# Window attention and box normalisation: x transposed in four equal pieces, 49 weight columns for the values, both normalisations moved

## The chip, the cores and the metric

The kernel runs on one core of a Trainium2 chip. The metric is device time in microseconds, the median of the runs. Such a core has a matrix engine (TensorE, PE in the profile, with its weight loads as PEld), VectorE (DVE), ScalarE (ACT), GpSimd (POOL) and a queue engine SyncE (SP), which issues the transfers. They work in parallel, each through its own instructions in order, and meet by semaphores. TensorE writes to PSUM, which is split in banks.

## The reference

x has 32 images of 56 x 56 tokens with 96 channels. Two layers, each with a residual.

```python
# _gn: group normalisation, 32 groups of 3 channels, over a whole image
x = x + attention(_gn(x))      # layer 1
x = x + box_layer(_gn(x))      # layer 2

# attention: x rolled by (-3, -3), cut into 64 windows of 7 x 7 = 49 tokens
qkv = xw @ qkv_w.T + qkv_b                     # 12 heads of 8 channels
attn = einsum(q * d**-0.5, k) + bias + mask    # 49 x 49 for each window and head
out = softmax(attn) @ v;  out = out @ proj_w.T + proj_b     # rolled back

# box_layer: s = x summed over 5 neighbours along a row
num = box_sum(s * s, channels, 20)
denum = box_sum(box_sum(x * x, row, 5), channels, 20) * count
out = nan_to_num(num / denum, nan=1.0)
```

## The kernel before

The order of all work is written out by hand. Every engine runs the same loop over slots (`for s in range(FIRST_SLOT, END_SLOT + 1)`, from -78 to 1070). A step j is a pair of windows; its scores are computed in slot j - 1. A unit U is one row of windows (four steps, four slots), an image is eight units (32 slots), and a group G is eight rows of image tokens in layer 2, seven to an image. The constants at the top (lines 44 to 53) say in which slot, counted from the start of a unit or an image, each piece of work stands: `units(s, V_AT)` gives the unit whose values are due in slot s, and so on. All pieces of a unit thus recur every four slots, and a slot is named below by its number modulo 32, or modulo 4 where it is the same in every unit.

Work of one unit on its way: `load` (SP) brings 112 x 4 x 96 tokens into one of eight `tok_in` tiles. `turn_x` (TensorE, line 377, L387) transposes them into bankA in four pieces, three of 112 tokens and one of 56. ScalarE's `keep_x` (L627) copies them to X, VectorE takes statistics (L869), and GpSimd splits X into a high and a low bf16 part, XH and XL (L991, L997). `qk` (L394 to L396) projects into bankB and bankC with the weights WH and WL, in three bf16 products each. ScalarE and VectorE split the results again (L635, L637; low_q L821, low_k L827), and SP's `stage` copies them into KS, QS and KE (L317, L325, L330), two units at a time. `values` (line 417, L436) computes v with 64 columns of XH or XL as weights at a time, although a window has 49 tokens: 48 products a unit, into the two halves of bankA; `keep_v` (L646) copies them.

Each step runs through `scores` (L454), `add_bias` (VectorE, L808), `maximum` (L815), `shift` (GpSimd, L1036), `turn_scores` (L466), `exponentials` (ScalarE, L656) and `times_v` (L481). For each unit follow `invert_sums` and `divide_o` (L838, L845), `turn_o` (L494), `keep_o` (L665), `project_o` (L504, into bankB) and `add_residual` (L857).

Layer 2 of a group: `normalise` to Y (ScalarE, L733), three sums on GpSimd (L1001, L1006, L1013), `square` and `square_box` (ScalarE, L740, L747), `deep_squares` (L549), `wide_squares` and `deep_y` (L555, L566), `invert` (L760, L763), `scale_squares`, `scale_boxes` and `ratio` (VectorE, L887, L894, L900), `turn_x1` (L575), `result` (L907), `store`. They stand in slots Y_AT to STORE_AT, four slots apart for successive groups.

Each normalisation is a chain across engines with links in fixed slots: aggregate (VectorE, L876), mean (L510) and variance (L515) on TensorE, deviation (L676 to L680), root (L687, L689) and scale (L699 to L713) on ScalarE. The first goes on to the weights: `norm_weights` multiplies them by the scale (L522, in bankA, the last work of TensorE's slot), `high_weights` on ScalarE writes the high part (L720, L724), and `fold` on VectorE the low part (L881, L882). `fold` comes first in VectorE's slot, ahead of `add_bias`.

What sets the order around the change: bankA passes in every unit from `values` (slot 0 modulo 4) to `turn_x` (slot 2) to `turn_o` (slot 3), and a normalisation's link uses it after the values have been kept. bankB passes between `qk` (slot 1), `deep_squares` (slot 2), `wide_squares` (slot 3) and, after `ratio` has read it, `project_o` (slot 0). `qk` waits for `add_residual` to have read bankB. TensorE's order in a slot is scores, times_v, values, turn_x, turn_o, turn_scores, turn_x1, project_o, qk, deep_squares, wide_squares and deep_y, and last the normalisation's links.

Of the kernel before, what the change touches and what calls it, by code (L numbers as in the profile page):

```python
# [8 lines left out]
BF16 = mybir.dt.bfloat16  # L9
ALU = mybir.AluOpType  # L10
# [33 lines left out]
LOAD_AT, FILL_AT, STATS_AT, HIGH_AT, LOW_AT = -78, -50, -49, -27, -27  # L44
# [4 lines left out]
Y_AT, PAIR_AT, FOUR_AT, BOX_AT = 45, 46, 47, 48  # L49
SQ_AT, DEEP_AT, WIDE_AT, RATIO_AT, OUT_AT, STORE_AT = 49, 50, 51, 52, 53, 54  # L50

NORM1 = dict(aggr=-21, mean=-20, dev=-20, var=-19, root=-19, scale=-18, weights=-16, high=-16, fold=-15)
NORM2 = dict(aggr=39, mean=40, dev=40, var=41, root=41, scale=42)
# [74 lines left out]
def build(nc, x, wT, bias_row, pT, pb_row, flipped, consts, out):  # L128
    ctx = ExitStack()
    with ctx:  # L130
# [20 lines left out]
        WH = sb("WH", [C + 1, 2 * C], BF16)  # L151
        WL = sb("WL", [C + 1, 2 * C], BF16)
# [143 lines left out]
        def _(sp):  # L296
# [43 lines left out]
            sp.dma_start(K[:, :], consts).then_inc(consts_in, 16)  # L340
            for U in range(UNITS):
                load(U)
# [8 lines left out]
            sp.wait_ge(pool_fills, 1)  # L351
# [23 lines left out]
        def _(pe):  # L375

            def turn_x(U):
# [7 lines left out]
                for t in range(4):  # L385
                    n = 2 * SIDE if t < 3 else SIDE
                    mm = pe.transpose(bankA[0:C, 2 * SIDE * t:2 * SIDE * t + n], tok_in[U % LOADS][0:n, t, :],  # L387
                                      roll[0:n, 0:n])
                mm.then_inc(xT_made, 1)

            def project(dst, col, u, done):

                xs = slice(TOK * u, TOK * u + TOK)
                pe.matmul(dst[0:C, 0:TOK], WH[:, col:col + C], XH[:, xs], start=True, stop=False)  # L394
                pe.matmul(dst[0:C, 0:TOK], WH[:, col:col + C], XL[:, xs], start=False, stop=False)
                pe.matmul(dst[0:C, 0:TOK], WL[:, col:col + C], XH[:, xs], start=False, stop=True  # L396
                          ).then_inc(done, 1)

            def qk(U):
# [9 lines left out]
                project(bankB, 0, u, q_made)  # L409
# [5 lines left out]
                project(bankC, C, u, k_made)  # L415

            def values(U):
# [10 lines left out]
                for w in range(2):  # L428
                    for p in range(PAIRS):
                        at = TOK * u + L * (2 * p + w)  # L430
                        xh, xl = XH[:, at:at + 64], XL[:, at:at + 64]
                        col = (2 * p + w) * C // 2
                        for part, (lhs, rhs) in enumerate(((xh, WHV), (xh, WLV), (xl, WHV))):
                            for h in range(2):
                                wv = rhs[m % 2][:, :].rearrange("c (a h d) -> c a h d", h=2, d=D)
                                mm = pe.matmul(bankA[64 * h:64 * h + 64, col:col + C // 2], lhs, wv[:, :, h, :],  # L436
# [179 lines left out]
        def _(act):  # L616
# [98 lines left out]
            def high_weights(m):  # L715
                act.wait_ge(norm_pe[0], PE_LINKS[0] * m + 3)
                if m:

                    act.wait_ge(k_made, UNITS * m)
                norm_link(m, 0, 13, act.activation(WH[:, :], bankA[0:C + 1, 0:2 * C], ACT.Copy))  # L720
# [370 lines left out]
```

## Time and profile before

| | us |
|---|---|
| median of 3 runs | 3615.91 (3614.39 to 3616.12) |
| profiled execution, its own time | 3616.91 |
| its span | 3615.1 |
| TensorE busy | 3343.9 (92%) |
| VectorE busy | 2800.6 (77%) |
| ScalarE busy | 2400.4 (66%) |
| GpSimd busy | 2276.4 (63%) |
| granted TensorE clock, mean | 0.988 |

The busy times say how much work each engine has, not which of them sets the end. The row of 40 slices says that the work is even from the second slice to the last but two. For the path one has to look at the timeline of one unit: which instruction starts late, and which engine it has waited for. In the timeline a row gives the start, the duration (of all instructions merged in the row, to the end of the last), the engine, the line, output <- input, shapes, the count, and in brackets the idle time before it with what ended it.

### The profile page before, as it was taken

What the parts mean: (1) busy time and instruction counts of PE and PEld (TensorE: products, weight loads), DVE (VectorE), ACT (ScalarE), POOL (GpSimd) and SP (SyncE); (2) the same over time, 40 slices, a digit from 0 to 9 for tenths busy, and PEclk for the clock granted to TensorE, in tenths of its full rate; (3) what the DMA queues carried; (4) which work ended last, traced back from release to release, by engine and by line L of the source; (5) the groups of instructions that cost most, each with busy time, mean ns of one, the idle gap of its engine ahead of it and who ended that gap; (6) DMA issues with size and microseconds to landing.
All of it is one profiled execution on the core that took longest, in us unless ns stands there. A gap on an engine that the chain in (4) does not pass through costs nothing.

```text
span 3615.1 us, 146768 instructions
## 1 busy us (share of the span) xinstructions
PE 3343.9 (92%) x60544; PEld 2747.6 (76%) x60544; DVE 2800.6 (77%) x4882; ACT 2400.4 (66%) x4705; POOL 2276.4 (63%) x2514
## 2 busy tenths in 40 slices
PE   4999999999999999999999999999999999999997
PEld 3777777777777777777777777777777777777775
DVE  4777878778787778787787787787787877877773
ACT  2566666666766666666667666676666676666664
POOL 3566666666666666666666666666666666666653
PEclk9999999999999999999999999999999999999995
DMA  3333333333333333333333333333333333332220
GB/s 81 82 74 85 76 80 85 78 78 83 80 78 81 83 76 80 85 77 80 86 75 79 85 76 80 86 75 80 84 78 78 82 80 77 81 84 66 67 58 22
DMA packets 385692, 280.19 MB, mean 78 GB/s; under 512 B 261927, under 2 KB 384904, under 8 KB 385032
## 3 DMA queue, kind: packets, MB, share of 16 engines
q1 hardware_dynamic: 385032, 270.81, 30.7%
q8 instruction: 485, 7.95, 0.9%
q14 instruction: 175, 1.43, 0.1%
HBM read 39.35 MB, written 38.54 MB: 22 GB/s over the span
## 4 chain that ended last, share of the span: by engine, by line
PE 41%; DVE 29%; issue 16%; SPq 8%; ACT 5%; DMA 2%; DVEq 0%; POOL 0%; ACTq 0%; POOLq 0%
PE pS L454 6%; DVE T L808 6%; PE pO L481 6%; SPq L317 5%; PE pM L504 5%; PE pP L466 5%; PE pM L566 4%; DVE MX L815 4%; PE pM L555 4%; DVE X L857 3%; PE pM L494 3%; DVE O L845 3%; DVE numt L900 3%; DVE pM L887 3%; ACT qnh L635 3%
## 5 line engine op out<-in xcount | busy, mean ns | idle before, releaser
L1036 POOL TENSOR_TENSOR T<-T,MX 128x588 f32<-128x588 f32 x1024 | 1212.9, 1184 | 1235.7 <-DVE MX L815 1235.7
L808 DVE TENSOR_TENSOR T<-pS,table 128x588 f32<-128x588 f32 x1024 | 785.7, 767 | 526.1 <-PE pS L454 511.9
L466 PE MATMUL pP<-K,T 113*128 113x113 f32 x6144 | 806.8, 268 | 0.6 <-ACT P L656 0.3
L481 PE MATMUL pO<-V,P 128*49 128x18 f32 x24576 | 723.5, 197 | 80.2 <-DVE O L845 60.0
L481 PEld LDWEIGHTS pO<-V,P 128*49 128x49 f32 x24576 | 692.5, 126 | 118.2 <-issue 78.3
L815 DVE TENSOR_REDUCE MX<-T 128x12 f32<-128x588 f32 x1024 | 769.0, 751 | 2.1
L656 ACT ACTIVATE P<-pP 128x588 f32<-128x588 f32 x1024 | 674.6, 659 | 141.0 <-PE pP L466 116.6
L466 PEld LDWEIGHTS pP<-K,T 113*128 113x128 f32 x6144 | 612.9, 141 | 32.4 <-POOL T L1036 0.6
L646 ACT ACTIVATE V<-pM 49x384 f32<-49x384 f32 x512 | 264.0, 516 | 337.4 <-PE pM L436 331.2
L454 PE MATMUL pS<-KE,QS 128*64 128x196 bf16 (+1 forms) x8192 | 474.7, 234 | 12.6 <-DMA KE<-KS 11.8
L454 PEld LDWEIGHTS pS<-KE,QS 128*64 128x64 bf16 x8192 | 290.2, 109 | 232.1 <-issue 164.7
L627 ACT ACTIVATE X<-pM 96x392 f32<-96x392 f32 x256 | 135.5, 529 | 269.3 <-PE pM L387 269.3
L665 ACT ACTIVATE OT<-pM 96x392 f32<-96x392 f32 x256 | 126.1, 493 | 279.7 <-PE pM L494 277.6
L566 PEld LDWEIGHTS pM<-K,ybox 96*112 96x112 f32 x1792 | 218.1, 183 | 69.5 <-issue 5.9
L1013 POOL TENSOR_TENSOR ybox<-y,Y 96x448 f32<-96x448 f32 x224 | 254.8, 1137 | 17.6
L504 PE MATMUL pM<-OT,PT 97*96 97x392 f32 x512 | 222.3, 516 | 44.4 <-DVE numt L900 44.4
L997 POOL TENSOR_TENSOR XL<-X,XH 96x392 bf16<-96x392 f32 x256 | 238.1, 930 | 20.5
L1001 POOL TENSOR_TENSOR y<-Y 96x472 f32<-96x472 f32 x224 | 217.2, 970 | 39.4 <-ACT Y L733 39.4
L394 PE MATMUL pM<-XH,WH 97*96 97x392 bf16 x512 | 172.9, 338 | 73.4 <-DVE X L857 72.2
L436 PE MATMUL pM<-WHV,XL 97*64 97x48 bf16 x4096 | 226.1, 190 | 0.3 <-issue 0.3
L436 PE MATMUL pM<-WHV,XH 97*64 97x48 bf16 x4096 | 225.8, 190 | 0.6 <-issue 0.6
L436 PE MATMUL pM<-WLV,XH 97*64 97x48 bf16 x4096 | 225.8, 190 | 0.0
(93 smaller groups left out, 6142.8 us busy)
## 6 DMA issues: line engine op xcount, KB each, us to landing
KE<-KS SPq DMA_DIRECT2D x512, 147.0 KB, 2.9
KS<-knh SPq DMA_DIRECT2D x768, 49.0 KB, 2.0
QS<-qnh SPq DMA_DIRECT2D x768, 49.0 KB, 2.0
out<-tok_out SPq DMA_DIRECT2D x384, 84.0 KB
tok_in<-x SPq DMA_DIRECT2D x224, 84.0 KB
KS<-knl SPq DMA_DIRECT2D x384, 49.0 KB, 2.0
QS<-qnl SPq DMA_DIRECT2D x384, 49.0 KB, 2.0
tok_in<-x SPq DMA_DIRECT2D x224, 63.0 KB
```

What stands on the lines that cost most here:

```text
L436: mm = pe.matmul(bankA[64 * h:64 * h + 64, col:col + C // 2], lhs, wv[:, :, h, :], start=(part == 0), stop=(part == 2))
L454: mm = pe.matmul(pS[64 * w:64 * w + 64, bank, col:col + (h1 - h0) * L], Q[:, gq, at:at + 64], E[:, h0:h1, at:at + L], start=True, stop=True)
L466: mm = pe.transpose(pP[:, c, QN * at:QN * at + QN], T[j % 4][0:QN, 2 * h:2 * h + 2, :], pick)
L481: mm = pe.matmul(pO[64 * w:64 * w + L, col:col + VC], P32[j % 3][:, 2 * h + w, :], V[U % 2][:, 2 * p + w, h, :, :], start=True, stop=True)
L504: pe.matmul(bankB[0:C, 0:TOK], PT[:, :], OT[:, :], start=True, stop=True).then_inc(proj_made, 1)
L566: mm = pe.matmul(bankC[0:ROWS2, C * t:C * t + C], ybox2[:, ROWS2 * t:ROWS2 * t + ROWS2], band, start=True, stop=True)
L646: act.activation(V[U % 2][ps, :, :, h, 0:D], bankA[ps, 0:PAIRS * C].rearrange("p (w a d) -> p w a d", w=UNITS, d=D), ACT.Copy).then_inc(v_ ...
L656: act.activation(P32[j % 3][:, :, :].rearrange("p (c a w) q -> p c a (w q)", c=2, w=2), src, ACT.Exp).then_inc(p_made, 1)
L808: dve.tensor_tensor(T[j % 4][:, :, 0:L].rearrange("p (b h) k -> p b h k", b=2), pS[:, :, 0:HALF].rearrange("p b (h k) -> p b h k", k=L), t ...
L815: dve.tensor_reduce(MX[j % 4][:, :], T[j % 4][:, :, 0:L], AX.X, ALU.max).then_inc(maxed, 1)
L1013: pool.tensor_tensor(ybox[:, :].rearrange("c (r w) -> c r w", w=SIDE), y4[:, :, :], Y[:, :, 4:SIDE + 4], ALU.add).then_inc(ybox_step, 1)
L1036: pool.tensor_tensor(t, t, MX[j % 4][:, :].unsqueeze(2).broadcast_to([128, HEADS, L]), ALU.subtract).then_inc(shifted, 1)
```

## The change

Five edits:

- `turn_x` transposes four pieces of 112 tokens. The last piece has 56 tokens and 56 rows of the tile that no load writes; so GpSimd fills the eight `tok_in` tiles with zeros first, and SP waits for that before the first load.
- `values` takes 49 columns of XH or XL as weights instead of 64, and writes 49 rows of each half.
- The first normalisation, with load, turn_x and the statistics, stands four slots earlier. WH and WL, which it writes, become two buffers each.
- Layer 2 stands eight slots later, and so does the second normalisation, but for its aggregate.
- `high_weights` waits for the projections of the image before last instead of the last.

```diff
-LOAD_AT, FILL_AT, STATS_AT, HIGH_AT, LOW_AT = -78, -50, -49, -27, -27
+LOAD_AT, FILL_AT, STATS_AT, HIGH_AT, LOW_AT = -82, -54, -53, -27, -27
-Y_AT, PAIR_AT, FOUR_AT, BOX_AT = 45, 46, 47, 48
-SQ_AT, DEEP_AT, WIDE_AT, RATIO_AT, OUT_AT, STORE_AT = 49, 50, 51, 52, 53, 54
-NORM1 = dict(aggr=-21, mean=-20, dev=-20, var=-19, root=-19, scale=-18, weights=-16, high=-16, fold=-15)
-NORM2 = dict(aggr=39, mean=40, dev=40, var=41, root=41, scale=42)
+Y_AT, PAIR_AT, FOUR_AT, BOX_AT = 53, 54, 55, 56
+SQ_AT, DEEP_AT, WIDE_AT, RATIO_AT, OUT_AT, STORE_AT = 57, 58, 59, 60, 61, 62
+NORM1 = dict(aggr=-25, mean=-24, dev=-24, var=-23, root=-23, scale=-22, weights=-20, high=-20, fold=-19)
+NORM2 = dict(aggr=39, mean=48, dev=48, var=49, root=49, scale=50)
...
-        WH = sb("WH", [C + 1, 2 * C], BF16)
-        WL = sb("WL", [C + 1, 2 * C], BF16)
+        WH = [sb(f"WH{i}", [C + 1, 2 * C], BF16) for i in range(2)]
+        WL = [sb(f"WL{i}", [C + 1, 2 * C], BF16) for i in range(2)]
...
             sp.dma_start(K[:, :], consts).then_inc(consts_in, 16)
+            sp.wait_ge(pool_fills, LOADS)
             for U in range(UNITS):
                 load(U)
...
-            sp.wait_ge(pool_fills, 1)
+            sp.wait_ge(pool_fills, LOADS + 1)
...
                 for t in range(4):
-                    n = 2 * SIDE if t < 3 else SIDE
-                    mm = pe.transpose(bankA[0:C, 2 * SIDE * t:2 * SIDE * t + n], tok_in[U % LOADS][0:n, t, :],
-                                      roll[0:n, 0:n])
+                    at = 2 * SIDE * t
+                    mm = pe.transpose(bankA[0:C, at:at + 2 * SIDE], tok_in[U % LOADS][:, t, :], roll[0:2 * SIDE, :])
...
-                        xh, xl = XH[:, at:at + 64], XL[:, at:at + 64]
+                        xh, xl = XH[:, at:at + L], XL[:, at:at + L]
...
-                                mm = pe.matmul(bankA[64 * h:64 * h + 64, col:col + C // 2], lhs, wv[:, :, h, :],
+                                mm = pe.matmul(bankA[64 * h:64 * h + L, col:col + C // 2], lhs, wv[:, :, h, :],
...
-                if m:
-                    act.wait_ge(k_made, UNITS * m)
-                norm_link(m, 0, 13, act.activation(WH[:, :], bankA[0:C + 1, 0:2 * C], ACT.Copy))
+                if m >= 2:
+                    act.wait_ge(k_made, UNITS * (m - 1))
+                norm_link(m, 0, 13, act.activation(WH[m % 2][:, :], bankA[0:C + 1, 0:2 * C], ACT.Copy))
...
-            zero = [P32[0], XL, V[0], V[1], T[0], T[1], T[2], T[3], O[0], O[1], Y]
+            zero = [*tok_in, P32[0], XL, V[0], V[1], T[0], T[1], T[2], T[3], O[0], O[1], Y]
```

## Rows read from the trace of the kernel before

**Rows 1.** The page, busy time by engine.

```profile
PE 3343.9 (92%) x60544; PEld 2747.6 (76%) x60544; DVE 2800.6 (77%) x4882; ACT 2400.4 (66%) x4705; POOL 2276.4 (63%) x2514
```

**Rows 2.** Timeline of one plain unit, TensorE's and ScalarE's rows.

```profile
1441.99 0.34 PE L394 MATMUL pM<-XH,WH 97*96 97x392 bf16 x1 [0.19 <-DVE X L857]
...
1446.70 0.73 PE L481 MATMUL pO<-V,P 128*49 128x18 f32 x24
...
1449.88 0.46 PE L454 MATMUL pS<-KE,QS 128*64 128x196 bf16 x8
...
1452.91 0.87 PE L504 MATMUL pM<-OT,PT 97*96 97x392 f32 x2 [0.20 <-DVE numt L900]
...
1455.62 0.34 PE L394 MATMUL pM<-XH,WH 97*96 97x392 bf16 x1 [0.19 <-DVE X L857]
...
1456.32 0.49 ACT L635 ACTIVATE qnh<-pM 96x392 bf16<-96x392 f32 x1 [0.20 <-PE pM L396]
```

**Rows 3.** Timeline, TensorE, near the end, where nothing is loaded any more.

```profile
3423.77 0.73 PE L481 MATMUL pO<-V,P 128*49 128x18 f32 x24 [0.74 <-DVE O L845]
...
3437.40 0.73 PE L481 MATMUL pO<-V,P 128*49 128x18 f32 x24 [0.74 <-DVE O L845]
```

**Rows 4.** Timeline, TensorE: turn_o and turn_x, each with what follows.

```profile
1502.45 0.59 PE L494 MATMUL pM<-K,O 113*96 113x113 f32 x4
...
1502.88 0.74 PE L466 MATMUL pP<-K,T 113*128 113x113 f32 x6
...
1512.97 0.68 PE L387 MATMUL pM<-K,tok_in 112*96 112x112 f32 x4
...
1513.58 0.80 PE L466 MATMUL pP<-K,T 113*128 113x113 f32 x6
```

**Rows 5.** Timeline, TensorE: first and last of the values' products.

```profile
1505.79 0.20 PE L436 MATMUL pM<-WHV,XH 97*64 97x48 bf16 x2
...
1506.52 0.20 PE L436 MATMUL pM<-WHV,XL 97*64 97x48 bf16 x2
```

**Rows 6.** Timeline, TensorE: slot 16, with the first normalisation's weights.

```profile
1517.27 0.46 PE L454 MATMUL pS<-KE,QS 128*64 128x196 bf16 x8
...
1519.60 0.82 PE L504 MATMUL pM<-OT,PT 97*96 97x392 f32 x2
...
1520.27 0.70 PE L522 MATMUL pM<-WT,DG 97*97 97x288 f32 x2
```

**Rows 7.** Timeline, ScalarE: from the high weights to slot 17's projection.

```profile
1521.17 0.31 ACT L720 ACTIVATE WH<-pM 97x192 bf16<-97x192 f32 x1
...
1524.32 0.49 ACT L635 ACTIVATE qnh<-pM 96x392 bf16<-96x392 f32 x1 [0.56 <-PE pM L396]
```

**Rows 8.** Timeline, ScalarE: slot 9 with its links, and a group's normalise.

```profile
1454.44 0.75 ACT L733 ACTIVATE Y<-X,g 96x448 f32<-96x448 f32 x1
...
1497.77 0.49 ACT L635 ACTIVATE qnh<-pM 96x392 bf16<-96x392 f32 x1 [0.20 <-PE pM L396]
```

**Rows 9.** Timeline, TensorE: a unit early on, without group work.

```profile
160.38 0.73 PE L481 MATMUL pO<-V,P 128*49 128x18 f32 x24 [0.91 <-DVE O L845]
...
171.85 0.73 PE L481 MATMUL pO<-V,P 128*49 128x18 f32 x24 [0.92 <-DVE O L845]
```

**Rows 10.** Timeline, TensorE: two successive groups after the last attention work.

```profile
3561.93 1.81 PE L549 MATMUL pM<-K,SQ 96*112 96x96 f32 x8 [3.22 <-ACT SQ L740]
...
3568.97 1.78 PE L549 MATMUL pM<-K,SQ 96*112 96x96 f32 x8
```

**Rows 11.** Timeline of the start, GpSimd and SP.

```profile
8.14 0.78 POOL L1042 MEMSET O<- 128x384 f32 x2
...
1.22 8.11 SPq L305 DMA_DIRECT2D tok_in<-x  x18
```

**Rows 12.** Timeline, TensorE; then one stretch: length, busy us by engine, PEclk, DMA.

```profile
3367.20 0.73 PE L481 MATMUL pO<-V,P 128*49 128x18 f32 x24 [1.34 <-DVE O L845]
...
3368.70:3375.50 6.80, 6.80 (x94) 5.10 (x92) 1.84 (x3) 3.14 (x6) 4.40 (x5) 0.50 0.28 68
```

More of the change, by code:

```diff
@@ L385, in turn_x, with project @@
                 for t in range(4):
-                    n = 2 * SIDE if t < 3 else SIDE
-                    mm = pe.transpose(bankA[0:C, 2 * SIDE * t:2 * SIDE * t + n], tok_in[U % LOADS][0:n, t, :],
-                                      roll[0:n, 0:n])
+                    at = 2 * SIDE * t
+                    mm = pe.transpose(bankA[0:C, at:at + 2 * SIDE], tok_in[U % LOADS][:, t, :], roll[0:2 * SIDE, :])
                 mm.then_inc(xT_made, 1)
-            def project(dst, col, u, done):
+            def project(dst, col, m, u, done):
                 xs = slice(TOK * u, TOK * u + TOK)
-                pe.matmul(dst[0:C, 0:TOK], WH[:, col:col + C], XH[:, xs], start=True, stop=False)
-                pe.matmul(dst[0:C, 0:TOK], WH[:, col:col + C], XL[:, xs], start=False, stop=False)
-                pe.matmul(dst[0:C, 0:TOK], WL[:, col:col + C], XH[:, xs], start=False, stop=True
+                pe.matmul(dst[0:C, 0:TOK], WH[m % 2][:, col:col + C], XH[:, xs], start=True, stop=False)
+                pe.matmul(dst[0:C, 0:TOK], WH[m % 2][:, col:col + C], XL[:, xs], start=False, stop=False)
+                pe.matmul(dst[0:C, 0:TOK], WL[m % 2][:, col:col + C], XH[:, xs], start=False, stop=True
                           ).then_inc(done, 1)
@@ L408, in qk @@
                     pe.wait_ge(ql_made, U)
-                project(bankB, 0, u, q_made)
+                project(bankB, 0, m, u, q_made)
                 G = group_of(U - QK_AHEAD - 1)
@@ L414, in qk @@
                     pe.wait_ge(kl_made, U)
-                project(bankC, C, u, k_made)
+                project(bankC, C, m, u, k_made)
             def values(U):
@@ L880, in fold @@
                 dve.wait_ge(norm_act[0], ACT_LINKS[0] * m + 14)
-                dve.tensor_tensor(WL[:, :], bankA[0:C + 1, 0:2 * C], WH[:, :], ALU.subtract).then_inc(folded, 1)
+                dve.tensor_tensor(WL[m % 2][:, :], bankA[0:C + 1, 0:2 * C], WH[m % 2][:, :], ALU.subtract).then_inc(folded, 1)
                 dve.tensor_tensor(WLV[m % 2][:, :], bankA[0:C + 1, 2 * C:3 * C], WHV[m % 2][:, :], ALU.subtract
```

## The prediction

> **What bounds the kernel now.** I read the busy table first. TensorE is busy 92% of the span [rows 1], so the obvious reading is that every nanosecond taken from it is a nanosecond gained. The other views say otherwise. The waits view shows TensorE itself waiting on VectorE in three places of each group of four slots, so I followed one such unit (four slots, one row of windows) in the timeline by engine.
>
> [rows 2] are one plain unit. The first projection L394 starts at 1441.99 and again at 1455.62: a unit is 13.63 us. Between them the path is this. L394 to L396 fill bankB, ScalarE's L635 follows, then VectorE runs without a pause through low_q, add_bias, low_k, the maximum, the reciprocal and divide_o, and `times_v` (L481, 1446.70) starts when divide_o is done. Then TensorE is the bound for 3.18 us, up to the scores at 1449.88. Then VectorE's add_bias and its three group operations (slot 0) let `project_o` (L504) go 3.03 us after those scores, with 0.20 us of TensorE idle before it. Then add_bias and add_residual let L394 go, with 0.19 us idle before it. From the scores of slot 0 to L635 it is 6.44 us.
>
> So two of the four slots are set by VectorE with TensorE waiting at their end, and these are exactly the places where `values` (slot 0, ahead of L504) and `turn_x` (slot 2, ahead of the wait for divide_o) stand. The trace has a natural experiment: in the last images nothing is loaded, so `turn_x` is absent. [rows 3] show two such L481 at 3423.77 and 3437.40: 13.63 us again, with 0.74 us of idle before each. Taking `turn_x` away as a whole bought nothing; its time became idle.
>
> **The change, part by part.**
>
> *x turned in four equal pieces.* Four transposes of turn_o (113 moving columns each, all of one shape) take 0.43 us from their start to the start of the next group, L466; turn_x with its short last piece takes 0.61 us [rows 4]. Made equal it should take some 0.43: 0.18 us less TensorE time per unit, 46 us over 256. The Trainium skill (TensorEngine Tiling (Array Packing), Key Properties) says that a change of tiling mode drains the engine; the 56-row piece among 112-row pieces fits, and the trace agrees with its 0.18 us. By that rule with TensorE as the bound the sum would be 46 us lower; by rows 3 it is worth nothing in a plain unit. I take zero, and the idle before L481 is the cover.
>
> *49 instead of 64 weight columns.* The 48 products of `values` start between 1505.79 and 1506.52 [rows 5]: 31.7 ns for each pair (one of each half). L481, with weights of 49 fp32 columns, has 24 in 0.73 less its last one's 0.20 us [rows 2], 46 ns a pair. If fp32 weights pass twice, 98 passes cost 46 and 64 cost 31.7, so 15 fewer save about 6 ns a pair, 0.14 us a unit. Bounds: 0 (the pace is one of issue) to 0.18 (in proportion to the columns). In plain units it lies ahead of L504's wait and gives nothing. It counts only where slot 0 has no group work: there L504 follows straight on (below).
>
> *The two normalisations.* Both wait chains move among other work, and here lies the sum for an image of eight units. Slots are counted modulo 32; each image has seven groups, so one unit is free of deep_squares, wide_squares, turn_x1 and the VectorE group steps. Before, that free unit (slots 14 to 17) also holds the first normalisation's weights (slot 16) and fold (17). In [rows 6], slot 16 opens at 1517.27, L504 needs no VectorE result and starts 2.33 us later, norm_weights (L522) follows after 0.67, and the fold's wait for L720 and L724 pushes L635 to 1524.32 [rows 7]: 7.05 us instead of 6.44, that is +0.61. After the change weights and fold stand in slots 12 and 13, where the groups run. norm_weights stands behind project_o in TensorE's queue, and project_o waits for VectorE's ratio. So L504 starts at 3.03, L522 at 3.70, ends at 4.40, and L720 starts at 4.43 instead of 3.90. From L720 to L635 the rows have 3.15 us (fold, add_bias and add_residual behind it on VectorE, then L394): 7.58 against 6.44, **+1.14 us**. Behind the waiting fold are queued add_bias, the residual and the maximum, so TensorE's L394 and GpSimd's shift wait too. The second WH buffer takes away a wait for k_made that would appear only by moving; qk's own wait for the fold was never alone at the end, since add_residual behind the fold ends later.
>
> The freed unit (now slots 22 to 25) loses the weights: slot 24 to L635 is 0.70 shorter than a plain one (2.33 against 3.03) and `values` counts there: -0.70 - 0.14. In slots 22 and 23 it saves what it saved before (slots 14 and 15).
>
> The mean of the first normalisation moves from slot 12 to 8, that of the second from 8 to 16. Each lengthens TensorE's slot by its two small products as before: no change. But the free SQ and Y places move too. Slot 9 after holds the deviation links and both the square and the normalise of groups. Before, slot 9 held the links and one of them, and L635 had 0.20 us of slack behind its exponentials [rows 8]. One more activation of 0.75 (0.65 with the overlap of successive ones) less 0.20 and less the overlap of 0.10 at its own start delays L635 by 0.35, and from there VectorE's chain to L481: **+0.35**. Slot 17 (second normalisation) has the square alone: nothing.
>
> Sum per steady image: 0.35 + 1.14 - 0.61 - 0.70 - 0.14 = +0.04 us; over the 29 images with both groups and a next image, +1 us. With nothing for 49 columns it is +5, with 0.18 it is 0.
>
> *Second layer eight slots later.* Two units at the front run without group work, two more at the end consist of it alone. A unit without groups is 11.47 us [rows 9], 2.16 less than a plain one: -4.3 us. Without groups slot 0 is TensorE's own, so 0.14 counts in the 14 or so such units: -2.0 us. At the end a lone group takes 7.04 us, from one L549 to the next [rows 10]: +14.1 us. The stores in SP's queue move with the groups; the staging copies behind them are issued in the same order within four slots, and nothing on TensorE waits for them in the plain unit.
>
> *The start.* SP now waits until GpSimd has filled the eight tok_in tiles. A fill of about this size takes 0.39 us (two O tiles in 0.78), eight of them 3.1, and GpSimd begins within the first microsecond, so the loads that began at 1.22 begin near 3.9 [rows 11]: +2.7 us, and SP issues without a pause until the first staging, so it passes through. The normalisation four slots ahead puts one more turn_x between the weights and the first projection, at half clock twice 0.43: +0.9. The additional load ahead of the first staging (two issues) fits into SP's wait for low_k.
>
> **Sum.** +1.2 (steady) - 4.3 - 2.0 + 14.1 + 2.7 + 0.9 = +12.6 us on the profiled execution (3616.9 us; its span 3615.1, the median of the runs 1.0 lower): 3629.5, or **3629 us** against the median of 3615.9, +0.35%. What the change takes from TensorE (0.32 x 256 = 82 us) goes almost wholly into waiting.
>
> **Rivals.**
>
> A. *As worked out* (0.60): own range 3618 to 3642. The ends are the bounds of the 49 columns (+6, -2), a normalisation cost wrong by 0.25 us an image (7 us), and the ends of the kernel by 2 us.
>
> B. *TensorE is the bound after all*: the 82 us are gained and the ends cost 11: about 3545. For it speaks the 92%; against it the 13.63 us without turn_x. 0.04.
>
> C. *The fold hides in its new place*: if L522 does not wait behind project_o's ratio, or VectorE has room, the 1.14 goes and with it 33 us: 3596. For it: the first normalisation has four slots more before `qk` needs it. Against it: the fold blocks its own in-order queue, whatever the reader's distance. 0.12.
>
> D. *The middle*: the halves of C, or ends that cost less (the two lone groups partly beside the last attention work): within 0.2% of before, 3609 to 3623. 0.12.
>
> E. *Slower, by the clock.* The TensorE that does less waits longer before L481. In [rows 12] an idle of 1.34 us there is followed by 6.8 us at the 1.2 GHz level, while 0.92 [rows 9] is not. The Trainium skill (TensorE: Matmul & The Clock Gate, Part 1) has the low clock as the state the engine falls back to when it is idle; the rows agree. The free unit stands at 0.74 now and would stand at 0.92, the group-free ones at 1.10. The mechanism decides once the fall comes in the free unit of every image: up to 3.4 us for each, 29 times, 3728; with falls half as long 3678. 0.12.
>
> **The numbers.** The range of 8 in 10 leaves out B, most of E's upper half and a little of C: 3596 to 3660. A measurement of this kernel can tell about 0.2% (7 us) from no change. Faster by more than that: B, C and a little of D, 0.18. Within: D and the low end of A, 0.19. Slower: most of A, and E: 0.63.
>
> **What would show it.** Right: plain units stay at 13.63 us; turn_x takes 0.43; the idle before L481 and L504 grows by 0.18 and 0.14; the fold waits longer for L724; slot 24 is shorter than slot 20; two more lone groups at the end; first scores near 74 us instead of 70. Wrong: plain units below 13.5 (then TensorE was the bound), slots 12 and 13 as long as 20 and 21 (C), the granted clock below one in mid-kernel (E).

## The result and the profile after

| | before | after |
|---|---|---|
| median of 9 runs, us | 3616.12 (3611.2 to 3629.3) | 3628.14 (3625.12 to 3632.86) |
| ratio of the two, 95% interval | | 1.0032 (1.0021 to 1.0043) |
| span of the profiled execution, us | 3615.1 | 3626.3 |
| granted TensorE clock, mean | 0.988 | 0.983 |

The kernel became slower by 0.32%; forecast was 0.35%. The mean clock differs by the two ends of the program: after, the granted clock is 0.50 from 61.4 to 78.5 us (before, the trace lists no clock ahead of 78.2) and from 3536.2 us to the end, before from 3539.3 to an end that comes 11.2 us earlier. The page of the changed kernel, to be read beside [rows 1]:

```profile
PE 3282.4 (91%) x60544; PEld 2713.9 (75%) x60544; DVE 2786.3 (77%) x4882; ACT 2385.1 (66%) x4705; POOL 2281.6 (63%) x2522
```

TensorE is busy 61.5 us less, with the same number of instructions, in a kernel that takes longer. The waits view of the same kernel has the waits that matter here (engine, line, whom it waited for: us, times, longest):

```profile
PE pO L481 <- DVE O L845: 140.8, 254, 1.6
...
DVE WL L881 <- ACT WHV L724: 51.7, 32, 3.5
...
PE pM L504 <- DVE numt L900: 45.6, 211, 0.6
```

The first of these was 60.0 us in 81 waits before, and is now a wait in nearly every unit. (The 0.14 us that TensorE idles there in a plain unit of before is too short for the views to list.) TensorE's timeline of one plain unit of after shows it; it answers to [rows 2] and [rows 4] (turn_x is L388 now):

```profile
1353.37 0.87 PE L504 MATMUL pM<-OT,PT 97*96 97x392 f32 x2 [0.21 <-DVE numt L900]
...
1356.07 0.34 PE L394 MATMUL pM<-XH,WH 97*96 97x392 bf16 x1 [0.19 <-DVE X L857]
...
1358.08 0.59 PE L388 MATMUL pM<-K,tok_in 112*96 112x112 f32 x4
1358.51 0.74 PE L466 MATMUL pP<-K,T 113*128 113x113 f32 x6
1359.09 0.94 PE L549 MATMUL pM<-K,SQ 96*112 96x96 f32 x8
1359.95 0.46 PE L454 MATMUL pS<-KE,QS 128*64 128x196 bf16 x8
1360.79 0.73 PE L481 MATMUL pO<-V,P 128*49 128x18 f32 x24 [0.37 <-DVE O L845]
```

turn_x takes 0.43 us to the next group, as forecast. From L394 to L481 it is 4.72 us, and in [rows 2] it was 4.71: all that TensorE saved there, 0.23 us, became idle, which grew from 0.14 to 0.37 us. The values' 48 products answer to [rows 5]:

```profile
1378.88 0.20 PE L436 MATMUL pM<-WHV,XH 97*49 97x48 bf16 x2
...
1379.49 0.20 PE L436 MATMUL pM<-WHV,XL 97*49 97x48 bf16 x2
```

26.5 ns a pair instead of 31.7, 0.13 us less in a unit. The whole image can be laid out as the distances between the scores (L454) of its slots, four slots to a unit. This table is the median over 25 images in the middle, worked out from the start times of L454 in the two traces:

| slots of the image | 0-3 | 4-7 | 8-11 | 12-15 | 16-19 | 20-23 | 24-27 | 28-31 | image |
|---|---|---|---|---|---|---|---|---|---|
| before | 13.63 | 14.10 | 13.72 | 12.30 | 14.24 | 13.63 | 13.63 | 13.63 | 108.88 |
| after | 13.63 | 14.10 | 13.98 | 14.78 | 13.72 | 12.21 | 12.81 | 13.63 | 108.85 |

A steady image takes the same time in both kernels; what the change costs is therefore paid at the ends of the program. The slow unit is now slots 12 to 15, where the first normalisation's weights and fold came in. Its rows in the timeline of after, TensorE, to be read beside [rows 6] and [rows 7]:

```profile
1392.05 0.46 PE L454 MATMUL pS<-KE,QS 128*64 128x196 bf16 x8
...
1395.07 0.87 PE L504 MATMUL pM<-OT,PT 97*96 97x392 f32 x2 [0.21 <-DVE numt L900]
1395.78 0.65 PE L522 MATMUL pM<-WT,DG 97*97 97x288 f32 x2
1396.36 0.46 PE L454 MATMUL pS<-KE,QS 128*64 128x196 bf16 x8
...
1398.92 0.34 PE L394 MATMUL pM<-XH,WH 97*96 97x392 bf16 x1 [0.85 <-DVE X L857]
```

and VectorE's of the same moment:

```profile
1397.11 0.36 DVE L881 TENSOR_TENSOR WL<-pM,WH 97x192 bf16<-97x192 f32 x1 [1.51 <-ACT WHV L724]
...
1397.55 0.76 DVE L808 TENSOR_TENSOR T<-pS,table 128x588 f32<-128x588 f32 x1
```

These rows show a queue across engines. project_o starts 3.02 us after the slot's scores because it waits for VectorE's ratio, norm_weights stands behind it, ScalarE's high parts behind that, and VectorE's fold (L881) keeps its engine waiting for 1.51 us with add_bias and the residual behind it, so that L394 finds 0.85 us of idle ahead.

At the end of the program the two further lone groups stand, 7.02 us apart, as in [rows 10]:

```profile
3539.11 1.78 PE L549 MATMUL pM<-K,SQ 96*112 96x96 f32 x8 [0.74 <-DVE X L857]
...
3546.13 1.78 PE L549 MATMUL pM<-K,SQ 96*112 96x96 f32 x8
```

### The profile page after: what moved, and what is told of

Read it like the earlier page. It is cut to its first block, busy times and chain, and to the rows that moved or that the text cites. A ratio compares the mean times of both kernels' runs of the same rounds, so it can differ in the third digit from the quotient of the medians.

```text
span 3626.3 us, 146802 instructions
## 1 busy us (share of the span) xinstructions
PE 3282.4 (91%) x60544; PEld 2713.9 (75%) x60544; DVE 2786.3 (77%) x4882; ACT 2385.1 (66%) x4705; POOL 2281.6 (63%) x2522
## 4 chain that ended last, share of the span: by engine, by line
PE 35%; DVE 30%; issue 16%; SPq 9%; ACT 6%; DMA 2%; POOL 0%; DVEq 0%; ACTq 0%; POOLq 0%
SPq L317 7%; DVE T L808 7%; PE pM L504 5%; PE pO L481 5%; PE pS L454 5%; DVE MX L815 4%; PE pM L566 4%; PE pM L555 4%; PE pP L466 4%; DVE O L845 3%; PE pM L494 3%; DVE numt L900 3%; DVE pM L887 3%; ACT qnh L635 3%; DVE X L857 3%
## 5 line engine op out<-in xcount | busy, mean ns | idle before, releaser
L481 PE MATMUL pO<-V,P 128*49 128x18 f32 x24576 | 723.3, 197 | 140.8 <-DVE O L845 140.8
L481 PEld LDWEIGHTS pO<-V,P 128*49 128x49 f32 x24576 | 693.3, 126 | 179.8 <-issue 129.7
L466 PE MATMUL pP<-K,T 113*128 113x113 f32 x6144 | 794.4, 265 | 1.2 <-ACT P L656 0.6
L656 ACT ACTIVATE P<-pP 128x588 f32<-128x588 f32 x1024 | 674.1, 658 | 151.2 <-PE pP L466 118.3
L466 PEld LDWEIGHTS pP<-K,T 113*128 113x128 f32 x6144 | 623.2, 141 | 18.3 <-issue 1.1
L454 PE MATMUL pS<-KE,QS 128*64 128x196 bf16 (+1 forms) x8192 | 474.4, 234 | 16.7 <-DMA KE<-KS 15.3
L454 PEld LDWEIGHTS pS<-KE,QS 128*64 128x64 bf16 x8192 | 290.5, 109 | 236.6 <-issue 165.2
L504 PE MATMUL pM<-OT,PT 97*96 97x392 f32 x512 | 221.4, 514 | 45.7 <-DVE numt L900 45.6
L394 PE MATMUL pM<-XH,WH 97*96 97x392 bf16 x512 | 171.5, 335 | 68.1 <-DVE X L857 67.8
L549 PE MATMUL pM<-K,SQ 96*112 96x96 f32 x1792 | 219.2, 267 | 4.7 <-ACT SQ L740 3.2
L566 PE MATMUL pM<-K,ybox 96*112 96x96 f32 x1792 | 217.5, 266 | 0.0
L821 DVE TENSOR_TENSOR qnl<-pM,qnh 96x392 bf16<-96x392 f32 x256 | 143.8, 562 | 91.8 <-ACT qnh L635 91.7
```

The costliest lines, as they stand in the source:

```text
L454: mm = pe.matmul(pS[64 * w:64 * w + 64, bank, col:col + (h1 - h0) * L], Q[:, gq, at:at + 64], E[:, h0:h1, at:at + L], start=True, stop=True)
L466: mm = pe.transpose(pP[:, c, QN * at:QN * at + QN], T[j % 4][0:QN, 2 * h:2 * h + 2, :], pick)
L481: mm = pe.matmul(pO[64 * w:64 * w + L, col:col + VC], P32[j % 3][:, 2 * h + w, :], V[U % 2][:, 2 * p + w, h, :, :], start=True, stop=True)
L504: pe.matmul(bankB[0:C, 0:TOK], PT[:, :], OT[:, :], start=True, stop=True).then_inc(proj_made, 1)
L566: mm = pe.matmul(bankC[0:ROWS2, C * t:C * t + C], ybox2[:, ROWS2 * t:ROWS2 * t + ROWS2], band, start=True, stop=True)
L656: act.activation(P32[j % 3][:, :, :].rearrange("p (c a w) q -> p c a (w q)", c=2, w=2), src, ACT.Exp).then_inc(p_made, 1)
```

## The experiments

Times are medians of one set of runs; each ratio is to the kernel before on the same chip, with its 95% interval. The kernel before took 3612.55 us beside the first four, 3613.49 beside the next three, 3614.06 beside the last two. The unit lengths of most of them stand in one table behind the fifth.

**One part alone: equal pieces** (in the kernel before).

```diff
+            sp.wait_ge(pool_fills, LOADS)
...
-                    n = 2 * SIDE if t < 3 else SIDE
-                    mm = pe.transpose(bankA[0:C, 2 * SIDE * t:2 * SIDE * t + n], tok_in[U % LOADS][0:n, t, :],
-                                      roll[0:n, 0:n])
+                    at = 2 * SIDE * t
+                    mm = pe.transpose(bankA[0:C, at:at + 2 * SIDE], tok_in[U % LOADS][:, t, :], roll[0:2 * SIDE, :])
...
-            zero = [P32[0], XL, V[0], V[1], T[0], T[1], T[2], T[3], O[0], O[1], Y]
+            zero = [*tok_in, P32[0], XL, V[0], V[1], T[0], T[1], T[2], T[3], O[0], O[1], Y]
```

> The kernel before, with the four equal pieces of turn_x alone (and the fills of tok_in and SP's wait that belong to them). Theory (plain units are bound by VectorE ahead of L481): TensorE saves 0.18 us a unit, the idle before L481 grows by as much, a plain unit stays at 13.63 us; only the later start of the loads shows, +2 to +3 us. Rival (TensorE is the bound): 46 us less, plus 3 for the start, so 43 us faster.

Measured: 3613.75 us, 1.0005 (0.9996 to 1.0014). TensorE's timeline of this kernel, the place of turn_x:

```profile
1443.45 0.59 PE L388 MATMUL pM<-K,tok_in 112*96 112x112 f32 x4
1443.88 0.75 PE L466 MATMUL pP<-K,T 113*128 113x113 f32 x6
...
1446.16 0.73 PE L481 MATMUL pO<-V,P 128*49 128x18 f32 x24 [0.37 <-DVE O L845]
```

turn_x is 0.18 us shorter, the wait behind it is 0.23 us longer (0.37, in the kernel before 0.14), the unit stays at 13.63. TensorE as the bound would have given some 43 us; that rival has fallen. The later start shows as 1.2 us, less than the 2 to 3 expected and not clear of zero.

**One part alone: 49 columns** (in the kernel before).

```diff
-                        xh, xl = XH[:, at:at + 64], XL[:, at:at + 64]
+                        xh, xl = XH[:, at:at + L], XL[:, at:at + L]
...
-                                mm = pe.matmul(bankA[64 * h:64 * h + 64, col:col + C // 2], lhs, wv[:, :, h, :],
+                                mm = pe.matmul(bankA[64 * h:64 * h + L, col:col + C // 2], lhs, wv[:, :, h, :],
```

> The kernel before, with 49 weight columns for the values alone. Theory: 0.14 us a unit less on TensorE, which counts only in the units without group work (14 at the front and the free unit of 29 images, whose ScalarE chain starts at the end of the values): 4 to 7 us faster in all; plain units stay at 13.63 us with the idle before L504 at 0.34 instead of 0.20. Rival (TensorE is the bound): 0.14 x 256 = 36 us faster.

Measured: 3611.04 us, 0.9994 (0.9985 to 1.0003): 1.5 us at the median, no difference that the interval can tell from none. The trace says where it counts and where not. In the steady images slots 16 to 19 are 0.12 us shorter (14.12 for 14.24), the one unit in which project_o waits for no VectorE result; every other unit is unchanged. An image is 0.13 us shorter. The idle before L504 was expected to grow to 0.34; it stayed:

```profile
1435.60 0.54 PE L575 MATMUL pM<-K,X 96*112 96x96 f32 x4
1436.35 0.87 PE L504 MATMUL pM<-OT,PT 97*96 97x392 f32 x2 [0.21 <-DVE numt L900]
```

Here turn_x1 (L575), the work just ahead, starts 0.73 us after the L466 in front of it, and 0.64 us in the kernel before: it took up most of the time itself.

**The schedule alone**: the changed kernel with the old turn_x and the old values (and without the fills and the wait for them).

```diff
-                    at = 2 * SIDE * t
-                    mm = pe.transpose(bankA[0:C, at:at + 2 * SIDE], tok_in[U % LOADS][:, t, :], roll[0:2 * SIDE, :])
+                    n = 2 * SIDE if t < 3 else SIDE
+                    mm = pe.transpose(bankA[0:C, 2 * SIDE * t:2 * SIDE * t + n], tok_in[U % LOADS][0:n, t, :],
+                                      roll[0:n, 0:n])
...
-                        xh, xl = XH[:, at:at + L], XL[:, at:at + L]
+                        xh, xl = XH[:, at:at + 64], XL[:, at:at + 64]
```

> The changed kernel with turn_x and values as they were before: the move of the normalisations and of layer 2, with the second WH and WL, alone. Theory: +14 us at the end, +1 at the start, -4 for two units without groups, and per steady image +1.14 (weights and fold among the groups) +0.35 (slot 9) -0.61 -0.70, so +0.2 us x 29 = +5: 16 us slower than before in all. Rival (the moves gain, and something else in the change costs): no change or faster.

Measured: 3629.0 us, 1.0045 (1.0033 to 1.0058), 16 us above its before. So the loss is the schedule's. The two savings on TensorE give back about 4 us of it (1.0032 against 1.0045, in intervals that overlap). No run moves only layer 2 or only the first normalisation; what each of the two costs is read from the unit table and the rows.

**What the saving would be worth with TensorE as the bound.** The theory says that VectorE's divide_o decides when times_v may start. In VectorE's queue the reciprocal and divide_o stand behind the maximum of the next step, and nothing in the data requires that. The same edit in both kernels:

```diff
+                for U in units(s, O_AT):
+                    invert_sums(U)
+                    divide_o(U)
                 for j in steps(s + 1):
                     maximum(j)
...
-                for U in units(s, O_AT):
-                    invert_sums(U)
-                    divide_o(U)
```

In the kernel before:

> The kernel before, with invert_sums and divide_o ahead of maximum in VectorE's slot instead of behind it; no work is added or removed. Theory (VectorE's chain to divide_o bounds slots 1 to 3): divide_o comes 0.67 us earlier, times_v at once behind its scores, a plain unit falls by the 0.31 us that TensorE idles there, to 13.3; the free unit and the one with the last statistics of x1 by 0.67. In all 3.2 us an image and some 9 us at the front: 100 us faster, 3515. Rival (TensorE's throughput is the bound, waits are bookkeeping): an order on VectorE changes nothing, within 5 us of before.

Measured: 3553.74 us, 0.9844 (0.9829 to 0.986). VectorE's timeline of this kernel, with divide_o ahead of the maximum:

```profile
1419.39 0.56 DVE L845 TENSOR_TENSOR O<-pO,rden 128x384 f32<-128x384 f32 x1
1419.86 0.76 DVE L815 TENSOR_REDUCE MX<-T 128x12 f32<-128x588 f32 x1
```

and TensorE's:

```profile
1420.16 0.46 PE L454 MATMUL pS<-KE,QS 128*64 128x196 bf16 x8
1420.45 0.70 PE L481 MATMUL pO<-V,P 128*49 128x18 f32 x24
```

L481 follows 0.29 us behind the scores and waits for nothing. In the changed kernel:

> The changed kernel, with invert_sums and divide_o ahead of maximum. Theory: divide_o is no longer last; now TensorE's path through slots 1 to 3 is, and the 0.18 us of the equal pieces becomes time: a plain unit falls from 13.64 to 13.15 (0.49), the free unit and the one with the last statistics by 0.67; 4.3 us an image, about 130 us in all, 3495. So with this order the change gains against the old kernel in the same order (about 20 us), though it lost 12 without it. Rival (TensorE bound): no change to the changed kernel, 3628.

Measured: 3501.34 us, 0.9688 (0.9675 to 0.9701). One unit of it, TensorE:

```profile
1309.23 0.34 PE L394 MATMUL pM<-XH,WH 97*96 97x392 bf16 x1 [0.19 <-DVE X L857]
...
1322.28 0.34 PE L394 MATMUL pM<-XH,WH 97*96 97x392 bf16 x1 [0.19 <-DVE X L857]
```

13.05 us. Units as in the table above, for all kernels but two: equal pieces alone has the units of before, and the first attempt of the best of both, below, is told in words:

| slots | 0-3 | 4-7 | 8-11 | 12-15 | 16-19 | 20-23 | 24-27 | 28-31 | image |
|---|---|---|---|---|---|---|---|---|---|
| before | 13.63 | 14.10 | 13.72 | 12.30 | 14.24 | 13.63 | 13.63 | 13.63 | 108.88 |
| 49 columns alone | 13.63 | 14.10 | 13.72 | 12.30 | 14.12 | 13.63 | 13.63 | 13.63 | 108.75 |
| schedule alone | 13.63 | 14.10 | 13.97 | 14.77 | 13.72 | 12.21 | 12.93 | 13.63 | 108.95 |
| before, divide_o first | 13.28 | 13.42 | 13.55 | 11.63 | 14.70 | 13.28 | 13.28 | 13.28 | 106.43 |
| after | 13.63 | 14.10 | 13.98 | 14.78 | 13.72 | 12.21 | 12.81 | 13.63 | 108.85 |
| after, divide_o first | 13.05 | 13.43 | 13.45 | 14.33 | 13.32 | 11.54 | 13.07 | 13.05 | 105.24 |
| after, fold late | 13.63 | 14.10 | 13.97 | 14.22 | 13.73 | 12.21 | 12.81 | 13.63 | 108.30 |
| after, both | 13.05 | 13.42 | 13.45 | 13.67 | 13.32 | 11.54 | 13.07 | 13.05 | 104.57 |
| before, all but schedule, high first | 13.05 | 13.42 | 13.32 | 11.63 | 13.52 | 13.05 | 13.05 | 13.05 | 104.08 |

The plain unit tells the theory's point: the order alone is worth 0.35 us (13.28). With the equal pieces it is 0.23 more (13.05), all of it in slot 2, where turn_x stands (3.02 us to 2.79), of a piece that was worth nothing as long as VectorE decided. The miss of the first of the two, 59 us where 100 were expected, sits in slots 16 to 19 (14.70 where 14.24 had been) and in four images of 29 that are 3.0 to 4.6 us longer, each with a stretch at a granted clock of 0.50. The second came near in time (3501.34 us for 3495), but with 3.6 us an image where 4.3 were expected. It misses in slots 24 to 27, which became 0.26 us longer (13.07 for 12.81) instead of shorter. There VectorE's low_q waits long for ScalarE's L635, which follows a square, a normalise and the exponentials:

```profile
1389.68 0.56 DVE L821 TENSOR_TENSOR qnl<-pM,qnh 96x392 bf16<-96x392 f32 x1 [1.70 <-ACT qnh L635]
```

**The fold's place.** In the changed kernel the fold stands ahead of add_bias in slot 13. Put behind result (L907), ahead of low_k:

```diff
-                for m in images(s, NORM1["fold"]):
-                    fold(m)
...
+                for m in images(s, NORM1["fold"]):
+                    fold(m)
                 for U in units(s, QK_AT + 1):
                     low_k(U)
```

> The changed kernel, with fold behind add_bias, add_residual and result in VectorE's slot 13 instead of first. Theory (most of the 1.14 us is the fold that blocks VectorE's queue until ScalarE's L724): the wait is gone, what stays is L522 on TensorE (0.48) and the fold's own 0.53 less 0.24 of idle before low_q: 0.8 instead of 1.14, 10 us faster than the changed kernel (3618). Rival (the cost is norm_weights behind project_o on TensorE alone): no change, 3628.

Measured: 3609.34 us, 0.9988 (0.9979 to 0.9997). VectorE's timeline:

```profile
1390.95 0.54 DVE L907 TENSOR_TENSOR tok_out<-pM,numt 112x384 f32<-112x384 f32 x1
1391.42 0.34 DVE L881 TENSOR_TENSOR WL<-pM,WH 97x192 bf16<-97x192 f32 x1
1391.68 0.24 DVE L882 TENSOR_TENSOR WLV<-pM,WHV 97x96 bf16<-97x96 f32 x1
```

The wait of 1.51 us is gone, the unit is 14.22 instead of 14.78, and 29 images of 0.55 us are 16 us, more than the 10 that were expected. The fold's own 0.44 us of work is still in VectorE's slot 13, so what the unit lost is the wait at that place in the queue. The 0.59 us that stay are mostly norm_weights behind project_o on TensorE: slot 12 is still 0.48 us longer than in a plain unit. This is half of the forecast's rival C (which had the whole 1.14 gone), made true by another order, and it is enough to take the loss of the change away.

**The best of both, first attempt**: the kernel before with equal pieces (and their fills and wait), 49 columns and divide_o first, and the old schedule.

```diff
-                    n = 2 * SIDE if t < 3 else SIDE
-                    mm = pe.transpose(bankA[0:C, 2 * SIDE * t:2 * SIDE * t + n], tok_in[U % LOADS][0:n, t, :],
-                                      roll[0:n, 0:n])
+                    at = 2 * SIDE * t
+                    mm = pe.transpose(bankA[0:C, at:at + 2 * SIDE], tok_in[U % LOADS][:, t, :], roll[0:2 * SIDE, :])
...
-                        xh, xl = XH[:, at:at + 64], XL[:, at:at + 64]
+                        xh, xl = XH[:, at:at + L], XL[:, at:at + L]
...
+                for U in units(s, O_AT):
+                    invert_sums(U)
+                    divide_o(U)
                 for j in steps(s + 1):
                     maximum(j)
...
-                for U in units(s, O_AT):
-                    invert_sums(U)
-                    divide_o(U)
```

> The kernel before with all that should gain and none of the moves: equal pieces, 49 columns, invert_sums and divide_o ahead of maximum; the schedule of slots is that of before. Theory: e4's 100 us, and 0.18 us more in the six plain units of each image (31 us) and 6 for the columns, less 3 at the start: 3480, faster than the changed kernel in the same order by about 15. Rival (the moved schedule is worth something once VectorE's order is right): slower than the changed kernel in that order.

Measured: 3567.78 us, 0.9875 (0.9859 to 0.989), nearly 90 us worse than expected (the profiled execution, at 3556.61, is the fastest of the four). Two things are in the trace. First, ScalarE's timeline, at the end of slot 16 and the start of slot 17:

```profile
1489.63 0.58 ACT L747 ACTIVATE ybox<-ybox 96x448 f32<-96x448 f32 x1 [0.68 <-POOL ybox L1013]
1490.11 0.31 ACT L720 ACTIVATE WH<-pM 97x192 bf16<-97x192 f32 x1
```

and VectorE's, behind it:

```profile
1490.73 0.36 DVE L881 TENSOR_TENSOR WL<-pM,WH 97x192 bf16<-97x192 f32 x1 [2.81 <-ACT WHV L724]
```

The high weights stand behind square_box (L747) in ScalarE's queue, which waits for GpSimd's last sum; the fold waits 2.81 us for them, and TensorE behind the fold. Second, TensorE's timeline right after:

```profile
1492.55 0.34 PE L394 MATMUL pM<-XH,WH 97*96 97x392 bf16 x1 [1.80 <-DVE X L857]
...
1494.81 1.16 PE L481 MATMUL pO<-V,P 128*49 128x18 f32 x24
```

and the windows view of two stretches (from and to; length; busy us and instructions of PE, PEld, DVE, ACT, POOL; granted clock, DMA):

```profile
1486.00:1493.20 7.20, 5.40 (x118) 4.02 (x114) 4.23 (x8) 5.45 (x11) 4.85 (x7) 0.98 0.28 70
1493.20:1500.00 6.80, 6.80 (x71) 5.88 (x70) 3.40 (x6) 2.65 (x5) 4.49 (x5) 0.52 0.54 132
```

After the 1.80 us of idle the clock stands at its lower level, 1.2 GHz, and times_v takes 1.16 us instead of 0.70. Of 29 images 6 have the undisturbed 105.05 us, 8 have 106.6, 8 have 108.15, and 7 have 109.1 to 112.3: together 72 us more than 29 undisturbed ones. That is the mechanism of the forecast's rival E, a fall of the clock behind an idle stretch, in a kernel that it was not written for and behind another stretch than the one it named.

**The changed kernel with both orders** (divide_o first, fold late).

```diff
-                for m in images(s, NORM1["fold"]):
-                    fold(m)
...
+                for m in images(s, NORM1["fold"]):
+                    fold(m)
                 for U in units(s, QK_AT + 1):
                     low_k(U)
...
+                for U in units(s, O_AT):
+                    invert_sums(U)
+                    divide_o(U)
                 for j in steps(s + 1):
                     maximum(j)
...
-                for U in units(s, O_AT):
-                    invert_sums(U)
-                    divide_o(U)
```

> The changed kernel with both orders on VectorE: invert_sums and divide_o ahead of maximum, and fold behind result in slot 13. Theory: the two gains are of different places and add. The late fold took 0.66 us out of slot 13 (and gave 0.09 back in slot 15, where divide_o was last; now it isn't): 0.66 x 29 = 19 us below the version with divide_o first alone, 3482. Rival (both work on the same slack of VectorE): less than 5 us below it.

Measured: 3480.95 us, 0.9633 (0.9619 to 0.9648). The two gains add up.

**The best of both, second attempt**: the kernel of the first attempt, with the high weights ahead of square_box in ScalarE's queue.

```diff
+                for m in images(s, NORM1["high"]):
+                    high_weights(m)
                 for G in groups(s, BOX_AT):
                     square_box(G)
...
-                for m in images(s, NORM1["high"]):
-                    high_weights(m)
```

> The kernel before with equal pieces, 49 columns, divide_o ahead of maximum (as in the run that fell to the 1.2 GHz level in 22 of its images), and high_weights ahead of square_box on ScalarE. Theory (the clock fell because TensorE idled 1.80 us ahead of L394 in slot 17, behind the fold): L720 starts when L522 ends, 1.0 us earlier, the idle falls to 0.8 and the falls of the clock with it; an image takes some 104.1 us (105.05 without a fall before), 3460 in all, faster than the changed kernel in any order. Rival (it is the short free unit, slots 14 to 16, that lets the clock fall): the falls stay, an image loses 2 us on average to them, 3530.

Measured: 3458.89 us, 0.957 (0.9554 to 0.9586). ScalarE's timeline, the same place:

```profile
1351.16 0.33 ACT L720 ACTIVATE WH<-pM 97x192 bf16<-97x192 f32 x1 [0.19 <-PE pM L522]
...
1351.81 0.58 ACT L747 ACTIVATE ybox<-ybox 96x448 f32<-96x448 f32 x1
```

TensorE's timeline:

```profile
1353.62 0.34 PE L394 MATMUL pM<-XH,WH 97*96 97x392 bf16 x1 [0.85 <-DVE X L857]
```

and the windows view from 200 to 3300 us:

```profile
200.00:3300.00 3100.00, 2973.57 (x56294) 2481.38 (x56292) 2566.46 (x4519) 2230.65 (x4360) 2103.15 (x2322) 1.00 0.34 83
```

Two instructions moved past one: the idle is 0.85 us, slots 16 to 19 take 13.52 us where the undisturbed ones of the first attempt took 14.47 (0.95 x 29 = 28 us), and the last line has the clock at 1.00, where the first attempt has 0.98. The 28 us and the 72 us are the difference between the two profiled executions (3554.8 and 3457.1) within 3 us. This kernel is 4.3% faster than the one before; the changed kernel was 0.3% slower. It keeps the old schedule and is 22 us faster than the changed schedule with both orders (3480.95), so the moves of the change are not what the best kernel needs.

## Why the prediction was right, and in which steps it was not

The sum of the prediction against what the two profiled executions show, in us:

| term | predicted | measured |
|---|---|---|
| first scores (start of loads, extra turn_x) | +3.6 | +2.9 (70.25 to 73.17 us) |
| first two images | -6.3 | -8.4 |
| the other 30 images | +1.2 | +1.1 |
| last scores to the end | +14.1 | +15.6 |
| sum | +12.6 | +11.2 |

The mechanism was right: plain units that VectorE bounds, the two normalisations that cancel over an image, and two lone groups that are paid at the end. That the sum came so near is in part luck, for the misses of its terms, told below, go both ways: 0.7, 2.1 and 1.4 us too high in the first scores, the first images and the steady images, and 1.3 and 1.5 us too low in the last image and at the end.

*The bound.* [rows 3] carried the forecast: where turn_x is absent, its time is idle and the unit as long. The equal pieces alone confirm it, and the order of divide_o shows the other side: only then the 0.23 us are gained. TensorE, busy 92% of the time, gave up 0.36 us in a unit for nothing, and VectorE, with 77%, gave 0.35 by the order of its work alone. The Trainium skill (Perfetto Trace Analysis, Identifying the Most-Contended Engine) has the engine with the highest occupancy as the one to optimise first, but does not take the matmuls' busy share as the measure of TensorE: there it takes the work done against the peak, and the busy share of the weight loads. The trace agrees with the warning, and by the loads TensorE stands at 76% beside VectorE's 77% [rows 1]: so near that the shares leave the choice open, and only the waits decide it.

*The pieces.* Predicted 0.18 us for turn_x, measured 0.18 to the next group. The plain unit shows 0.23 once TensorE is its bound (13.28 to 13.05), and the idle before L481 grew by as much, not by 0.18: the L466 behind turn_x is 0.05 us shorter too (0.58 to the next group in after, 0.64 in before). This is a term that was undersized, at no cost here. The Trainium skill (TensorEngine Tiling (Array Packing), Key Properties) says that changing the tiling mode drains the engine; the runs put 0.23 us on this one odd piece, which fits that rule, but no run separates such a drain from anything else in which the short piece differs.

*49 columns.* 0.13 us against 0.14. The step behind the 0.14, that fp32 weights pass twice, was an assumption: L481 with 49 fp32 columns takes 46 ns a pair, the values with 49 bf16 columns 26.5. The two differ in more than the type of the weights, so no run settles it. The idle before L504 did not grow as written; turn_x1 took most of the time up.

*The two normalisations.* By the unit table: slots 12 to 15 are 1.15 us longer than a plain unit (predicted 1.14). Slots 16 to 19 lose the 0.61 of the weights and gain 0.09 with the second normalisation's links; slots 20 to 23, the first half of the free unit, are 0.09 shorter than slots 12 to 15 were, which had the first's links. The links were forecast to cost the same wherever they stand, and these two cancel. The free unit's second half is 0.82 shorter than a plain one (predicted 0.84). Slot 9 costs 0.26 instead of 0.35: this is the one mis-sized term of the image. ScalarE's timeline of after:

```profile
1383.01 0.76 ACT L740 ACTIVATE SQ<-X,g 96x448 f32<-96x448 f32 x1
1383.67 0.75 ACT L733 ACTIVATE Y<-X,g 96x448 f32<-96x448 f32 x1
1384.32 0.64 ACT L656 ACTIVATE P<-pP 128x588 f32<-128x588 f32 x1
1384.86 0.48 ACT L635 ACTIVATE qnh<-pM 96x392 bf16<-96x392 f32 x1
```

and of before, to be read with [rows 8]:

```profile
1496.18 0.76 ACT L740 ACTIVATE SQ<-X,g 96x448 f32<-96x448 f32 x1
1496.91 0.66 ACT L656 ACTIVATE P<-pP 128x588 f32<-128x588 f32 x1
```

From L740 to L635 it is 1.85 us after and 1.59 before. The exponentials (L656) of before began 0.73 us behind the square, where an activation that follows at once begins 0.66 behind it: a second slack of 0.07, ahead of the one of 0.20 that was counted, was overlooked. The image came out at 108.85 against 108.88, so -0.03 us where +0.04 was forecast. Over the 29 steady images it is -0.2 us in all, not the +1.2 of the forecast. The +1.1 in the table comes from the last image, +1.3, where the kernel after has a stretch of 3.4 us at a granted clock of 0.50 (from 3498.6 us) and the kernel before none.

"The fold waits longer for L724" was wrong in its letter: L881 waits 1.51 us, and 2.44 in the kernel before. VectorE has group work ahead of it now, so its wait begins later; what counts is when it ends, measured from the slot's scores, and that is what the 1.14 was worked out from.

*The ends.* The two lone groups cost 14.0 us by the rows and the end 15.6 in all. The 1.6 between them are a fall of the clock. After, the granted clock is 0.50 from 3522.5 to 3525.9 us, behind 1.34 us of idle:

```profile
3522.10 0.89 PE L481 MATMUL pO<-V,P 128*49 128x18 f32 x24 [1.34 <-DVE O L845]
3522.92 0.99 PE L494 MATMUL pM<-K,O 113*96 113x113 f32 x4
```

and before, the same place with the same idle is followed by the full clock (here turn_o, behind L481, takes 0.59 us):

```profile
3526.50 0.73 PE L481 MATMUL pO<-V,P 128*49 128x18 f32 x24 [1.34 <-DVE O L845]
```

From the project_o (L504) of this unit to the next it is 13.39 us after and 11.79 before. The loads began at 3.66 us, predicted 3.9, 2.4 us later than before, but the first scores were only 1.9 us later in the kernel with the equal pieces alone: the 2.7 us of the forecast did not pass through whole. The first images gained 2 us more than predicted. In the first three units 1.5 us of the late start come back (1.0 with the equal pieces alone); the rest was not separated.

*Rival E.* It did not come true in the steady images. The free unit had idle of 1.15 us before L481, more than the 0.92 of the prediction: the schedule alone has 0.91 there where the kernel before has 0.74, and the equal pieces add 0.23, not 0.18:

```profile
1430.99 0.73 PE L481 MATMUL pO<-V,P 128*49 128x18 f32 x24 [1.15 <-DVE O L845]
```

and the windows view of after from 200 to 3300 us has a granted clock of 1.00, as the kernel before has. Behind 3300 us, ahead of the long stretch at the end, after has three stretches of 3.4 us at 0.50 and before one of 6.8 [rows 12].

*What my expectations of the experiments missed* was in three of them the same step: a new order on VectorE makes TensorE faster, and I costed the plain unit but not the stages where ScalarE then comes last. In the kernel before with divide_o first, and in the first attempt, these are slots 16 and 17, where ScalarE stands behind GpSimd; in the changed kernel with divide_o first it is slot 25. The late fold missed the other way, with 0.55 us for an expected 0.34. In the changed schedule the high weights lie in another slot and meet no such wait, and divide_o first was worth more there (0.9688 against 1.0032, 3.4%) than in the kernel before (1.6%).

## What to carry to other kernels

Before taking work from the busiest engine, look at what ends its last wait in each stage, and look for a place in the same trace where that work is already missing: its time is either gone there or idle. In an in-order queue the place of a waiting instruction can cost more than its work (the fold: 0.55 us of a unit by its place alone, with 0.44 us of work); here two moves of a few lines, divide_o ahead of the maximum and the high weights ahead of a square that waits, made savings on TensorE worth something, and parts of a change that lost 0.3% became a kernel that gains 4.3%. And each time the bound engine gets faster, cost the stages with rare work again, for they are the ones that turn late.

## What the hardware showed beyond that

The granted clock does not fall by the length of one idle stretch alone. In every steady image the first projection behind the fold (L394) has one of TensorE's longest waits, and the runs differ in it (29 images each):

| kernel | idle before L394 | images with it | followed by a fall |
|---|---|---|---|
| second attempt, and after | 0.85 us | all | none |
| before | 1.00 | all but one | none |
| before, divide_o first | 1.3 to 1.4 | 28 | 4 |
| the same, last image | 1.8 | 1 | 1 |
| first attempt | 1.8 to 2.0 | 27 | 23 |

These 28 falls begin within 1.8 us of the start of L394. TensorE's 1.15 us of idle before L481 in after was followed by none, and 1.34 us there by a fall in one place and not in another, above. In these runs falls are more frequent where the idle is longer, but the same row can go either way. This is the first attempt's timeline at 1387 us, in an undisturbed image; the same row at 1492 us, above, was followed by the fall:

```profile
1387.51 0.34 PE L394 MATMUL pM<-XH,WH 97*96 97x392 bf16 x1 [1.80 <-DVE X L857]
```

and this the row of the kernel before with divide_o first, in one of its four images with a fall:

```profile
1384.90 0.34 PE L394 MATMUL pM<-XH,WH 97*96 97x392 bf16 x1 [1.43 <-DVE X L857]
```

A fall cost 1.6, 3.1 or 4.7 us in most of the disturbed images. The Trainium skill (TensorE: Matmul & The Clock Gate, Part 1) has the half clock as the state of an engine that has been idle; the rows agree on the level (0.52 of full speed in the stretch above), and show in addition that an engine busy for 95% of the time (2952.8 of 3100 us in the first attempt) can meet it in mid-kernel, behind an idle stretch under 2 us.

The pair of products with 49 columns of weights and 48 moving columns goes at 26.5 ns, with 64 columns at 31.7: 0.35 ns for each column that each of the two halves loses.
